# Two attention layers: fp16 copy and low part of the probabilities made for two key tiles at a time

## The reference

```python
# layer 0 attention, x is layer-normed, context is (16, 128, 512)
q = einsum('oc,bcn->bon', Wq, x); kv = einsum('oc,bcm->bom', Wkv, context)
q, k, v = split_heads(...)               # 8 heads of 64
attn = softmax(einsum('bhdi,bhdj->bhij', q, k))
out = einsum('bhij,bhdj->bhid', attn, v)
x = x + einsum('oc,bcn->bon', Wout, out) + bout
# layer 1 attention: the same with 8 heads of 16, biases, rotary
# embedding of q and k, and scores / sqrt(16)
```

## Time and profile before

| | |
|---|---|
| time, median of 3 runs | 3264.57 us (3253.11 to 3277.23) |
| span of the profiled execution | 3264.8 us |
| attention of layer 0 | about 80 to 1060 us, 61.3 us per batch |
| attention of layer 1 | about 1730 to 2522 us, 47.6 us per batch (50.2 us in some) |
| PE, DVE, ACT, POOL busy | 76%, 70%, 56%, 55% of the span |

### The profile page before, as it was taken

The page is one execution under the profiler, slowest core; times in us unless marked ns, Lnnn a source line. Parts: engine busy times, 40 slices in busy tenths (PEclk is TensorE's granted clock), DMA queues, the critical chain, the costliest instruction groups (busy, mean ns, idle before and its releaser), DMA issues. The chain is left out here.

```text
span 3264.8 us, 41636 instructions
## 1 busy us (share of the span) xinstructions
PE 2477.9 (76%) x11034; PEld 962.1 (29%) x11062; DVE 2300.3 (70%) x3282; ACT 1842.6 (56%) x3160; POOL 1806.1 (55%) x1577
## 2 busy tenths in 40 slices
PE   2999999999999046676647888989888312999930
PEld 0333333333333023233221222222222311555510
DVE  4778878878877775675636999888996571666644
ACT  1888888888888012232225888888887301444410
POOL 1667767767767010110125889888887275333445
PEclk9999999999999568898876999899998556999975
DMA  4232222222220300000001111111110103777745
GB/s 111 54 61 57 48 60 58 49 60 59 49 57 18 154 14 1 0 0 0 0 24 36 36 31 31 35 31 31 35 29 7 55 1 105 245 244 241 242 143 171
DMA packets 145405, 219.01 MB, mean 67 GB/s; under 512 B 20232, under 2 KB 108808, under 8 KB 144144
## 3 DMA queue, kind: packets, MB, share of 16 engines
q1 hardware_dynamic: 130448, 175.83, 20.5%
q0 software_dynamic: 14848, 41.99, 4.7%
HBM read 125.41 MB, written 42.02 MB: 51 GB/s over the span
## 5 line engine op out<-in xcount | busy, mean ns | idle before, releaser
L354 POOL TENSOR_TENSOR a_p_l<-a_probs,a_p_h 128x512 f16<-128x512 f32 x1024 | 1190.5, 1175 | 416.7 <-ACT a_p_h L564 414.7
L631 DVE TENSOR_REDUCE a_negmax<-a_ps_max 128x1 f32<-128x512 f32 x1024 | 675.7, 682 | 106.7 <-PE a_ps_max L431 101.9
L558 ACT ACTIVATE a_probs<-a_ps_st 128x512 f32<-128x512 f32 x1024 | 593.6, 593 | 236.4 <-PE a_ps_st L43 228.5
L564 ACT ACTIVATE a_p_h<-a_probs 128x512 f16<-128x512 f32 x1024 | 635.2, 626 | 1.3
L465 PE MATMUL a_ps_o<-a_p_h,a_v_h 128*128 128x512 f16 x1024 | 402.9, 393 | 1.9 <-POOL a_p_l L354 1.9
L679 DVE RECIPROCAL a_sums<-a_sums 128x128 f32<-128x128 f32 x384 | 356.3, 938 | 20.1 <-ACT a_plain L576 20.1
L890 POOL TENSOR_TENSOR f_hl<-f_h,f_hh 128x2048 f16<-128x2048 f32 x16 | 65.1, 4071 | 375.5 <-ACT f_hh L994 375.5
L431 PE MATMUL a_ps_max<-a_k_st,a_q_st 48*128 48x512 f16 x512 | 210.9, 413 | 32.9 <-DVE a_negmax L631 16.6
L43 PE MATMUL a_ps_st<-a_q_st,a_k_st 68*128 68x512 f16 x512 | 208.7, 408 | 6.9 <-ACT a_probs L558 6.2
L467 PE MATMUL a_ps_o<-a_p_h,a_v_l 128*64 128x512 f16 x512 | 206.3, 403 | 0.0
L470 PE MATMUL a_ps_o<-a_p_l,a_v_l 128*128 128x512 f16 x512 | 205.8, 402 | 0.0
(11 more groups left out here) (293 smaller groups left out, 4717.7 us busy)
## 6 DMA issues: line engine op xcount, KB each, us to landing
s_raw<-in_guT SPq DMA_DIRECT2D x32, 768.0 KB, 5.7
m_y<-s_y SPq DMA_DIRECT2D x32, 768.0 KB, 4.8
a_k_hh<-a_qk_h SPq DMA_DIRECT2D x64, 256.0 KB, 5.1
a_ctx_in<-in_ctx SPq DMA_DIRECT2D x32, 256.0 KB, 2.6
a_q_hl<-a_qk_h SPq DMA_DIRECT2D x32, 256.0 KB, 4.4
a_q_hm<-a_qk_h SPq DMA_DIRECT2D x32, 256.0 KB, 4.7
a_q_hl<-a_qk_l SPq DMA_DIRECT2D x32, 256.0 KB, 5.0
a_k_lo<-a_qk_l SPq DMA_DIRECT2D x32, 256.0 KB, 5.0
```

Of the source, the lines that this page charges most:

```text
L354: pool.tensor_tensor(p_l[:, h % 2, j, :], probs[:, h % RAWS, j, :], p_h[:, h % 2, j, :], ALU.subtract).then_inc(p_split, 1)
L558: act.activation(probs[:, h % RAWS, j, :], ps_st[:, j % 2, :], ACT.Exp, scale=1.0 if L0 else DH1 ** -0.5).then_inc(exped, 1)
L564: act.activation(p_h[:, h % 2, j, :], probs[:, h % RAWS, j, :], ACT.Copy).then_inc(p_high, 1)
L631: dve.tensor_reduce(negmax[:, h % 2, t:t + 1], ps_max[:, t % 2, :], AX.X, ALU.max, negate=True).then_inc(maxed, 1)
```

## The change

ScalarE's copy to p_h and GpSimd's difference p_l are made for two key tiles at once, 128 x 1024 instead of 128 x 512. In each head ScalarE now runs exp 0, exp 1, exp 2, copy of tiles 0 and 1, exp 3, take_out, copy of tiles 2 and 3. GpSimd runs the difference of tiles 0 and 1, normalise where there is one, and the difference of tiles 2 and 3. The counts of the semaphores p_high and p_split go from four to two per head, and the waits for them are rewritten. The exponentials and all matmuls stay as they are, and what is computed is the same.

```diff
-            def low_probs(batch, h, j):
-                need(pool, p_high, KD * (H * batch[0] + h) + j + 1)
-                pool.tensor_tensor(p_l[:, h % 2, j, :], probs[:, h % RAWS, j, :], p_h[:, h % 2, j, :], ALU.subtract).then_inc(p_split, 1)
+            def low_probs(batch, h, i):
+                need(pool, p_high, 2 * (H * batch[0] + h) + i + 1)
+                two = slice(2 * i, 2 * i + 2)
+                pool.tensor_tensor(p_l[:, h % 2, two, :], probs[:, h % RAWS, two, :], p_h[:, h % 2, two, :], ALU.subtract).then_inc(p_split, 1)
...
-                    for j in range(KD):
-                        low_probs(batch, h, j)
+                    for i in range(KD // 2):
+                        low_probs(batch, h, i)
                         m, p = normalised(batch, h)
-                        if j == 0 and m is not None and exists(m):
+                        if i == 0 and m is not None and exists(m):
                             normalise(m[0], p)
...
-                need(pe, p_split, KD * g + j + 1)
+                need(pe, p_split, 2 * g + j // 2 + 1)
...
-                need(act, p_split, KD * (g - RAWS) + j + 1)
+                need(act, p_split, 2 * (g - RAWS) + j // 2 + 1)
...
-            def high_probs(batch, h, j):
+            def high_probs(batch, h, i):
                 g = H * batch[0] + h
-                need(act, weighted, KD * (g - 2) + j + 1)
-                need(act, exped, 4 * g + j + 1)
-                act.activation(p_h[:, h % 2, j, :], probs[:, h % RAWS, j, :], ACT.Copy).then_inc(p_high, 1)
+                two = slice(2 * i, 2 * i + 2)
+                need(act, weighted, KD * (g - 2) + 2 * i + 2)
+                need(act, exped, 4 * g + 2 * i + 2)
+                act.activation(p_h[:, h % 2, two, :], probs[:, h % RAWS, two, :], ACT.Copy).then_inc(p_high, 1)
...
-                        if j > 0:
-                            high_probs(batch, h, j - 1)
+                        if j == 2:
+                            high_probs(batch, h, 0)
...
-                    high_probs(batch, h, KD - 1)
+                    high_probs(batch, h, 1)
```

## The result

The changed kernel takes 3568.08 us (median of 4 runs, 3565.23 to 3575.10) against 3263.12 us before (4 runs, 3253.11 to 3277.23): a ratio of 1.0926, 95% interval 1.0893 to 1.0959. The forecast was 3560. The profiled run has a span of 3573.3 us against 3264.8, so 308.5 us have to be found.

A forecast was written before the change was run, and what follows sets the result against it. TensorE was taken to set the pace in layer 0, while waiting at times in layer 1. Layer 0's 241 us, layer 1's 56 and 2 at the attentions' ends gave 299 on 3264.8, said as 3560; range 3490 to 3640.

The forecast's parts named there:

- Prices: A 128x1024 copy takes 1.05 us, a difference 2.13; about 0.09 us saved per pair on ScalarE, 0.1 on GpSimd.
- Lateness of normalise in layer 0: Normalise waits behind its head's first paired difference; TensorE stalls at heads 6, 0, 2 and 3, 9.8 us per batch.
- E: The start of exp 2 in a head, from which the forecast counts times; normalise was to end at E + 4.95.
- The waits at heads 0 and 2: Layer 0, TensorE waiting to project the next tile because take_out waits for normalise: 1.35 us and 1.8 us.
- Clock in layer 0: Clock falls after waits at head 7 and project_out, costing 3.2 and 2.8 us, together 6.0 per batch.
- the row of 6.37: Earlier trace: project_out's eight matmuls took 6.37 us at low clock against 3.60 at full, giving the price 2.8.
- Layer 1: Only project_out is hit: 1.7 us more waiting and 2.0 if the clock falls, 15 x 3.7 = 56 us.
- the other waits are covered: Layer 1 waits besides project_out: probs has two buffers, and weigh_values comes more than 2 us behind its difference.
- the rival with a steady clock: Stalls come in both layers but the clock holds: 178 us more, 3442 us; chance 0.18.
- The rival of a low clock as long as in layer 1: Clock stays low 7.5 us instead of about 3 at two places in layer 0: 3700 us; chance 0.14.
- The half of the Trainium skill's rule: If Scalar or Vector aren't saturated but cause bubbles elsewhere, breaking up may help; ScalarE at 77% in layer 0.

The follow-up runs named there:

- e1: The changed kernel with normalise ahead of the first difference of its head in all heads of both layers, pairs kept: 3372.45 us.
- e5: The changed kernel with ScalarE's copies one tile at a time again, only GpSimd's difference for a pair: 3485.09 us.
- e6: The changed kernel with unused matmuls in layer 0's waits, 12 before head 7 step 2 and 14 before project_out: 3537.16 us.
- e7: The changed kernel with 9 unused matmuls before the transposes at head 3 of layer 1 and 9 before its project_out: 3484.30 us.
- e8: The kernel before with one unused VectorE instruction per batch of layer 1, ahead of the rotated low parts at head 2: 3331.92 us.
- e10: The kernel before with 6 unused matmuls ahead of the transposes at head 3 of layer 1: 3249.39 us, ratio 0.9933.

## Why the prediction was right, point by point

- **Prices: right.** Difference 2141 ns (2.13 said), copy 1050 ns (1.05).
- **Lateness of normalise in layer 0: right, in place and size.** Normalise ends at E + 4.96 (4.95 said), take_out starts at E + 4.99 (5.04), TensorE's step 2 at E + 8.71 (8.70), idle 2.96 us. The waits at heads 0 and 2 are 1.21 and 1.85 (1.35 and 1.8 said), that of project_out 3.58 (3.75), where the clock had not fallen just ahead of it. e1 shows the cause by taking it away.
- **Clock in layer 0: right in kind, too large.** I said 2.8 at project_out and 3.2 at head 7, 6.0 a batch. A fall costs some 1.7 (e5), and all falls together 74.6 - 71.5 = 3.1 a batch by e6. Project_out takes 5.40 and not 6.37 us, since the low clock lasts 3.4 us, not the length of all eight matmuls; the row of 6.37 stood behind a wait of 6.80 and was the wrong neighbour. There is a fall I had not seen, behind the 1.85 us wait of head 2; it costs nothing of its own, since the steps that it slows run into project_out's wait (2.0 us there and not 3.58). The batch that ends at 480.96 lacks it and takes 74.7 us all the same. Three falls, two paid: the four waits are 2.96 + 1.21 + 1.85 + 3.58 = 9.6 us, with two falls 13.1 of the 13.3 by which a batch grew. I had 15.8.
- **Layer 1: the step that failed.** I gave 1.7 for project_out's wait and 2.0 for the clock. The first was near: in e7 TensorE had nothing but added matmuls from the end of the last product (2215.70 + 0.38 = 2216.08) to project_out at 2218.85, 2.77 us against 0.80 before, 2.0 more. With the clock up (e7) a batch costs 50.4, 2.8 more than 47.6: these 2.0 and 0.74 at head 3. But I looked for the clock's fall at project_out, and wrote that the other waits are covered. That sentence is the failed step: I asked which waits for GpSimd's and ScalarE's results would grow, and not what GpSimd's new times do to VectorE. The wait for VectorE at head 3, already 1.72 us in the earlier trace rows, grew by 0.74, and since it lies where the clock had sometimes fallen, it now fell always, and stayed low for 20 to 24 us over two heads. That makes 56.3 - 50.4 = 5.9 us a batch for the clock, where I had 2.0, and 105 us in all where I had 56.
- **The total is closer than its parts.** Layer 0 with its last batch was put at 241 us and took 11.6 + 189.1 = 201 up to its last output projection; layer 1 at 56 and took 105. The errors of -40 and +49 cancel; that the total came within 8 us of the forecast is luck.
- **Rivals.** e6 and e7 took 31 and 84 us off the kernel. Added up (no run has both) that leaves 3453: about what the rival with a steady clock gave (3442). So its price was right, and its condition false. The rival of a low clock as long as in layer 1 was wrong for layer 0. The half of the Trainium skill's rule (Perfetto Trace Analysis, Optimizing Scalar/DVE Operations) that speaks for breaking up instructions of an unsaturated engine held: both engines have less work now, and the kernel is slower.

That VectorE is held while GpSimd's difference runs was read from traces, not tested by an experiment of its own; but the reading is the same everywhere. In the traces of all thirteen kernels layer 1's low part of the rotated tile (128x512) stands 404 times from 1740 us on. In 266 of them no tensor_tensor of GpSimd was running when it began, and it took 0.67 to 0.69 us. In the other 138 one was, and it took 0.73 to 1.77 us and ended 0.54 to 0.55 us after that one did: 15 times in the changed kernel and once in the one before. In e8, too, where GpSimd makes four short differences in a row from 2177.43, it ends 0.55 us after the first of them and not after the row. The Trainium skill (SBUF — State Buffer, section "SBUF: two separate sides") says that a VectorE operation with two SBUF inputs and a GpSimd operation that reads SBUF share a port pair as an exclusive lock, held for a whole instruction; these traces agree.

## What to carry to other kernels

Before grouping work on an engine that has idle time, write down what stands behind the first group in its queue and when its result is needed; a cheaper instruction that ends later costs the engine that sets the pace whatever of the lateness it can't cover (2.96 of the 3.6 us by which normalise was late at head 6, 1.21 at head 0), and moving the one awaited instruction ahead of the group gives it back (188 us here). Then list TensorE's longest waits in the trace of before, and ask for each whether another engine's new times can lengthen it: 0.74 us more at one of 1.72 us cost eight times as much, 5.9 us a batch, through the clock. Where such a wait can't be shortened, a few spare matmuls in it are worth a trial (0.7% in the kernel before, 84 us in the changed one).

## What the runs showed of the hardware that I had not expected

- The low clock lasted 3.4 us at each of layer 0's steady falls and 20 to 24 us in layer 1 of the changed kernel (14 to 17 us in that of the kernel before). Behind the wait in layer 0 TensorE was busy all of the time (3.40 of 3.40 us in the window from 659.60), in layer 1 18.68 of 20.30 us. Why it came back so much later in layer 1 I did not settle.
- Whether a wait drops the clock is not set by its length alone: 1.72 us did so in 4 of 14 batches of layer 1 of the kernel before, 1.74 to 1.85 in 9 of 14 of layer 0 of the changed kernel, 2.78 not at all for 439 us of e5 and then again. Behind the 2.45 us in layer 1 it fell in every batch.
- Six matmuls per batch that compute nothing (e10) shortened layer 1 from 706.9 to 694.5 us.
